# Mixture-of-experts weights: bias folded from row sums on GpSimd and VectorE instead of column sums on TensorE

## Chip, cores and metric

The kernel runs on 1 core of one Trainium2 chip. The metric is the device time of one execution in microseconds (us). Engines are called as in the profile: PE is TensorE, DVE is VectorE, ACT is ScalarE, POOL is GpSimd, SP is SyncE, which here only issues DMAs.

## The reference

64 batches of 256 tokens of width 256 pass through two residual layers: x1 = x + LN(att(LN(x), ctx) + LN(x))·gamma + beta, with attention without softmax (per head k'v from 120 context rows, then q·kv), and then

```
h2   = layernorm(x1)
top2 = top-2 of softmax(h2 @ gate_w.T)            # 16 experts
y_e  = relu(h2 @ expert_w[e].T + expert_b[e])     # expert_w: 16 x 256 x 256, float32
out  = x1 + sum over the two experts of weight * y_e
```

## The kernel before

**Two parts.** The dense part (to about 475 us) treats one batch per step. The second part (two passes of 144 tiles of 128 rows) gathers rows sorted by expert, multiplies each tile with its expert's matrix and scatters the result. Only the dense part's code is touched, with one wait count at the head of the second.

**The bias fold.** The rows that the expert matrices multiply are not the normalised h2 but rows of x1 shifted by `sigma - mean` (L873, L882). They sum to 256·sigma, so a vector u added to every row of an expert's matrix adds 256·sigma·u to its product. The kernel adds u = (bias - column sums of the matrix)/256, which brings the bias in and takes the shift out. So each expert's `we` (128 partitions x 2 halves x 256 columns; `we` holds all 16 side by side) needs its column sums over 256 rows, spread over 128 partitions, then one addition. After it the matrix is split for fp32r products: `we_head` is the rounded copy (ACT, L934), `we_rest` the difference, written over `we` (POOL, L573).

**How it is staged.** Every engine has its own in-order program, `step(s)`, called for s = 0, 1, ... (or from -1); semaphores hold the engines together, and nothing is reordered. In a step each engine works on several batches at once: `s` is in projection, `s-1` in attention, `s-2` in the second layernorm, `s-3` (called `f`) in expert choice and scatter. The order in `step` is the order on the engine. POOL's step `s` waits for x1 of batch `s-1` (L552), that is for the end of DVE's step `s`, so it runs beside DVE's step `s+1`. It does `context_rest(s+1)` (c_rest, L543), `x_beta` (L558), the small copies L582 to L587, and two indirect DMAs that scatter batch f's rows (L594). Between x_beta and the small copies stand the two pieces of the weights' preparation below.

**The weights' preparation,** in 8 pieces of 2 experts, one piece per step:
- SP loads pieces 0 to 3 in step 0 and 4 to 7 in step 1 (L394), 512 KB each.
- POOL adds the two halves of a piece (`we_sum`, L568), in steps 1 to 8.
- PE, in `sum_columns` (L732, steps 2 to 9), multiplies by a matrix of -1 (which sums over partitions and spreads the sum to all) and, by a matrix of ones, the bias in three bf16 parts (`be_rows`), into `ps_fold`, which is the bank of the transposes of h. So `transpose_h` waits for the fold of the step before (L656).
- DVE, in `fold_bias` (L1113, steps 3 to 10), adds ps_fold/256 to the piece.
- ACT makes the head in steps 3 to 10 (L934), POOL the rest in steps 4 to 11 (L573).
- The bias parts are made at the start: DVE clears `be_rows` (L977) and splits the bias (L979), SP writes them to DRAM and reads them back as rows (L385, L389), with waits in SP's queue.

**Functions and lines that the change and the prediction touch:** `prepare_experts` and `load` of SP; POOL's `step` (L549 to L598); PE's `transpose_h`, `sum_columns`, `step`; ACT's `step` (L932 to L934); DVE's `split`, `fold_bias`, `step`. Other DVE work of a step that the prediction names: moments L993, scores L1006, gaps L1016, onehot L1028, attention plus residual L1070, kv L1076, scaled L1090, first weights L1042, and x1 L1103, the last.

Of the kernel before, what the change touches and what calls it, by code (L numbers as in the profile page):

```python
# [25 lines left out]
P = 128  # L26
# [3 lines left out]
E = 16  # L30
# [24 lines left out]
WARM_TABLE, WARM_LOADS, WARM_BOUNDARY = 16, 20, 36  # L55
WE_PIECES = 8
RB = 4
LOG_EXP_SET = 6
# [80 lines left out]

def build(nc, x, ctx_t, wkv_t, wq_t, gate_t, we_t, bkv, be, bq, gamma, beta, out):  # L140
    bins = [nc.dram_tensor("bins0", [ROWS, ROW], F32, kind="Internal").ap(),
            nc.dram_tensor("bins1", [DUMP + 2 * E * P, FULL], F32, kind="Internal").ap()]

    be_dram = nc.dram_tensor("be_dram", [3, E * D], BF16, kind="Internal").ap()

    def parts_as_rows(dram):
        return dram.rearrange("n (p m) -> p n m", p=P)

    with ExitStack() as ctx:
        def sb(name, shape, dt=F32):  # L150
            return ctx.enter_context(nc.sbuf_tensor(name, shape, dt))
# [28 lines left out]
        we_rest = we[:].bitcast(F32R)  # L180
        we_sum = sb("we_sum", [P, 2, E * D // WE_PIECES])
        idle = sb("idle", [P, 2 * D], BF16)
        kv_bias = sb("kv_bias", [SC, 2 * D])
        be_in = sb("be_in", [P, E * D // P])
        be_rest = sb("be_rest", [P, 2, E * D // P])
        be_part = sb("be_part", [P, 3, E * D // P], BF16)
        bq_sb = sb("bq_sb", [P, KC])
# [55 lines left out]
        wkv = row_flat[:, 0:4 * D].rearrange("p (c n) -> p c n", c=KC)  # L243
        be_rows = row_flat[:, 4 * D:4 * D + E * D // 2].bitcast(BF16)
        put_at = sb("put_at", [P, V], I32)
# [24 lines left out]
        s_wrest = sem("weight_rests_ready")  # L270
        s_whalf = sem("weight_halves_added")
        s_wsum = sem("weight_column_sums_ready")
        s_fold = sem("weights_with_bias_ready")
# [6 lines left out]
        s_zero = sem("zeros_made")  # L280
        s_split = sem("bias_split_step")
        s_eb = sem("expert_bias_rows_placed")
        s_ebd = sem("expert_bias_parts_in_dram")
        s_init = sem("dram_fill_written")
# [70 lines left out]
        def piece(n):  # L355
            return slice(n * E * D // WE_PIECES, (n + 1) * E * D // WE_PIECES)

        block = ctx.enter_context(nc.Block())


        @block.sync
        def _(sp):
# [20 lines left out]
            load(Batch(2))  # L383
            sp.wait_ge(s_split, 5)
            sp.dma_start(parts_as_rows(be_dram), be_part[:]).then_inc(s_ebd, 16)  # L385
            load(Batch(3))
            sp.wait_ge(s_zero, 3)
            sp.wait_ge(s_ebd, 16)
            sp.dma_start(be_rows[0:65:32, :], be_dram).then_inc(s_eb, 16)  # L389

            def prepare_experts(step):

                for n in pieces(step, 4):
                    sp.dma_start(we[:, :, piece(n)],  # L394
                                 we_t.rearrange("(c p) n -> p c n", p=P)[:, :, piece(n)]
                                 ).then_inc(s_we[n], 16)
                if step >= LEAD - 4:

                    sp.wait_ge(s_const, 2)
                    q = step - (LEAD - 4)  # L400
                    spare = bins[0][SPARE + 4 * q * P:SPARE + 4 * (q + 1) * P, :].rearrange("(j p) d -> p j d", p=P)
                    sp.dma_start(spare[:, :, 0:D], zeros[:, 0:D].unsqueeze(1).to_broadcast([P, 4, D])
                                 ).then_inc(s_init, 16)
                    sp.dma_start(spare[:, :, D:ROW], pad_facts[:, 1, 4 * q:4 * q + 4, :]).then_inc(s_init, 16)
                if step == LEAD - 5:

                    sp.wait_ge(s_const, 2)
                    regions = bins[0][0:SPARE, :].rearrange("(r n) d -> n r d", n=REGION)
                    facts = pad_facts[:, 0].rearrange("p (r o) d -> p r o d", o=2)
                    for o, ends in enumerate((regions[0:PAD], regions[REGION - PAD:REGION])):  # L410
                        sp.dma_start(ends[:, :, 0:D], zeros[:, 0:D].unsqueeze(1).to_broadcast([P, E // 2, D])
                                     ).then_inc(s_init, 16)
                        sp.dma_start(ends[:, :, D:ROW], facts[:, :, o, :]).then_inc(s_init, 16)
# [69 lines left out]
        def _(pool):  # L483
# [63 lines left out]
            context_rest(Batch(0))  # L547

            def step(s):  # L549
                p = s - 1  # L550
# [10 lines left out]
                if s.c == 0:  # L561
                    make_pads()
                if s.c >= 1:
                    for n in pieces(s.c - 1, 1):
                        pool.wait_ge(s_we[n], 16)
                        if n >= 2:
                            pool.wait_ge(s_wsum, n - 1)
                        pool.tensor_tensor(we_sum[:, n % 2], we[:, 0, piece(n)], we[:, 1, piece(n)],  # L568
                                           ALU.add).then_inc(s_whalf, 1)
                if s.c >= 4:  # L570
                    for n in pieces(s.c - 4, 1):
                        pool.wait_ge(s_whead, n + 1)
                        pool.tensor_tensor(we_rest[:, :, piece(n)], we[:, :, piece(n)],  # L573
                                           we_head[:, :, piece(n)].bitcast(F32),
                                           ALU.subtract).then_inc(s_wrest, 1)
                f = s - 3
                if f.exists():
# [15 lines left out]
                    for t in range(NT):  # L593
# [3 lines left out]
                                ap=r[:, t, POS_COL:POS_COL + 1].bitcast(I32), axis=0),  # L597
                            in_offset=None).then_inc(s_row[f.buf(4)], 16)  # L598

            dense_steps(step, 0, NB + 3)  # L600
# [18 lines left out]
        def _(pe):  # L619
# [29 lines left out]
            def transpose_h(b):  # L649
# [3 lines left out]
                if b.c >= 2:  # L653
                    pe.wait_ge(s_gfold, 1)
                if b.c >= 3:
                    pe.wait_ge(s_fold, min(b.c - 2, WE_PIECES))  # L656
                for c in range(KC):
# [73 lines left out]

            def sum_columns(n, b):  # L732
                pe.wait_ge(s_whalf, n + 1)
                pe.wait_ge(s_ht, b.times(1, 1))
                if n == 0:
                    pe.wait_ge(s_eb, 16)
                pe.matmul(ps_fold, ones_bf[:], be_rows[:, piece(n)], start=True, stop=False)
                pe.matmul(ps_fold, minus_ones[:], we_sum[:, n % 2], start=False, stop=True).then_inc(s_wsum, 1)

            def step(s):  # L740
# [13 lines left out]
                if s.c == 1:  # L754
                    sum_gate_columns(s)
                if s.c >= 2:
                    for n in pieces(s.c - 2, 1):
                        sum_columns(n, s)
                if (s - 2).exists():
# [54 lines left out]

            pe.wait_ge(s_wrest, WE_PIECES)
            for k in range(2):
# [9 lines left out]
        def _(act):  # L826
# [80 lines left out]
            def step(s):  # L907
# [23 lines left out]

                for n in pieces(s.c - 3, 1):  # L932
                    act.wait_ge(s_fold, n + 1)
                    act.activation(we_head[:, :, piece(n)], we[:, :, piece(n)], ACT.Copy).then_inc(s_whead, 1)  # L934

# [38 lines left out]
        def _(dve):  # L974
            dve.memset(eps[:], EPS).then_inc(s_zero, 1)
            dve.memset(idle[:].bitcast(U32), 0).then_inc(s_zero, 1)
            dve.memset(be_rows.bitcast(U32), 0).then_inc(s_zero, 1)  # L977

            def split(src, rest, part, n):  # L979

                dve.tensor_copy(part[:, 0, :], src).then_inc(s_split, 1)
                dve.wait_ge(s_split, n + 1)
                dve.tensor_tensor(rest[:, 0, :], src, part[:, 0, :], ALU.subtract).then_inc(s_split, 1)
                dve.wait_ge(s_split, n + 2)
                dve.tensor_copy(part[:, 1, :], rest[:, 0, :]).then_inc(s_split, 1)
                dve.wait_ge(s_split, n + 3)
                dve.tensor_tensor(rest[:, 1, :], rest[:, 0, :], part[:, 1, :], ALU.subtract).then_inc(s_split, 1)
                dve.wait_ge(s_split, n + 4)
                dve.tensor_copy(part[:, 2, :], rest[:, 1, :]).then_inc(s_split, 1)

# [121 lines left out]

            def fold_bias(n):  # L1113
                dve.wait_ge(s_wsum, n + 1)
                part = we[:, :, piece(n)]
                dve.scalar_tensor_tensor(out=part, in0=ps_fold.unsqueeze(1).to_broadcast([P, KC, 2 * D]),
                                         scalar=1.0 / D, in1=part, op0=ALU.mult, op1=ALU.add).then_inc(s_fold, 1)

            def step(s):
# [7 lines left out]
                if s.c == 2:  # L1127
                    centre_gate()
                if s.c >= 3:
                    for n in pieces(s.c - 3, 1):  # L1130
                        fold_bias(n)
                if b.exists():
# [43 lines left out]

            dve.wait_ge(s_be_in, 16)
            split(be_in[:], be_rest, be_part, 0)
            dense_steps(step, -1, NB + 3)


# [132 lines left out]
```

## Time and profile before

| | us |
|---|---|
| median of 3 runs | 890.44 (888.53 to 893.2) |
| profiled execution, span from first to last instruction | 888.4 |
| PE, DVE, ACT, POOL busy in it | 756.4, 684.9, 593.1, 602.5 |
| dense part, first scores to last | about 24 to 475 |

The profiled execution's own time is shown as its span alone; it lies 2.0 us below the median of the runs. A row of a timeline gives start, duration, engine, line, operation, output<-input with shapes, the count of merged instructions, and in brackets the engine's idle time before it and what ended it. Records of one engine overlap by some tens of nanoseconds, since the next instruction is taken up before the last has drained.

### The profile page before, as it was taken

To read this page: it belongs to the slowest core of one execution; us is meant where nothing else is said; L and a number is where in the kernel's file an instruction comes from. 1 tells how busy PE (TensorE), PEld (TensorE's weight loads), DVE (VectorE), ACT (ScalarE), POOL (GpSimd) and SP (SyncE) were. 2 spreads that over 40 slices of the span, in tenths; PEclk is the share of its full clock that TensorE was granted. 3 is DMA by queue.
4 is the path that set the end of the run, shared out by engine and by line. 5 is a ranking of instruction groups with operands and counts; after the bars stand their busy time and mean duration, and the time that the engine had idled before them with its cause. 6 is when DMAs were issued, how large, how long until landed. Compare 5 with 4: busy or idle time off the path is not lost.

```text
span 888.4 us, 21064 instructions
## 1 busy us (share of the span) xinstructions
PE 756.4 (85%) x5479; PEld 659.0 (74%) x5480; DVE 684.9 (77%) x2219; ACT 593.1 (67%) x1658; POOL 602.5 (68%) x776
## 2 busy tenths in 40 slices
PE   5998899999999999999988777787777899777750
PEld 4866688888888888888875777786665898667750
DVE  4989999999999999999994767777662575554540
ACT  4877789989989989889872545555452565454440
POOL 4578766666666666666662777777774677777775
PEclk9999999999999999999997999999998999999995
DMA  7426456676676776676513898999996999999941
GB/s 241 151 71 166 148 184 207 219 238 203 222 237 200 227 234 202 223 236 199 197 50 99 283 307 297 310 300 310 303 303 203 350 363 343 302 305 293 305 154 77
DMA packets 137626, 205.77 MB, mean 232 GB/s; under 512 B 38962, under 2 KB 74290, under 8 KB 137546
## 3 DMA queue, kind: packets, MB, share of 16 engines
q1 hardware_dynamic: 113101, 130.72, 47.7%
q0 software_dynamic: 24448, 74.14, 22.3%
q8 instruction: 34, 0.56, 0.3%
q14 instruction: 43, 0.35, 0.1%
HBM read 87.99 MB, written 116.81 MB: 231 GB/s over the span
## 4 chain that ended last, share of the span: by engine, by line
DVE 37%; issue 24%; POOL 11%; PE 11%; DMA 10%; SPq 4%; ACT 1%; POOLq 0%; DVEq 0%; ACTq 0%
POOL out_rows L609 8%; DVE st L993 6%; DVE x L1103 6%; DVE scaled L1090 5%; DVE att L1070 4%; DMA row_in<-bins 4%; DMA bins<-row_in,put_at 4%; DVE kv L1076 4%; POOL bins L609 3%; DVE top_i L1023 3%; DMA out_rows<-xh,put_at 2%; DVE scores_top L1011 2%; SPq L459 2%; PE ps_q L679 1%; DVE scores_top L1006 1%
## 5 line engine op out<-in xcount | busy, mean ns | idle before, releaser
L609 POOL DMA_INDIRECT out_rows<-xh,put_at x143 | 145.2, 1015 | 57.6 <-issue 39.9
L609 POOL DMA_INDIRECT bins<-row_in,put_at x143 | 143.8, 1006 | 57.7 <-issue 37.9
L594 POOL DMA_INDIRECT bins<-rows x128 | 127.1, 993 | 72.0 <-POOL rows L587 47.5
L679 PE MATMUL ps_q<-h_t,wq 128*128 128x256 f32 x512 | 133.3, 383 | 0.0
L543 POOL TENSOR_TENSOR c_rest<-c_sb,c_head 128x240 fp32r<-128x240 f32 x64 | 44.8, 700 | 87.2 <-DVE x L1103 84.1
L679 PEld LDWEIGHTS ps_q<-h_t,wq 128*128 128x128 f32 x512 | 92.8, 191 | 13.6 <-ACT h_t L899 0.4
L798 PE MATMUL ps_q<-we_head,row_head 128*128 x288 | 87.3, 303 | 8.6 <-DVE row_rest L1234 8.6
L1261 DVE SCALAR_TENSOR_TENSOR row_in<-row_in 128x256 f32<-128x256 f32 x144 | 63.3, 480 | 28.8 <-ACT row_in L955 28.2
L858 ACT ACTIVATE q_t<-ps_q,bq_sb 128x256 f32<-128x256 f32 x128 | 60.4, 472 | 36.5 <-PE ps_q L679 36.5
L558 POOL TENSOR_TENSOR x_beta<-xh,beta_sb 128x512 f32<-128x512 f32 x64 | 81.9, 1280 | 0.8 <-DVE x L1103 0.8
L701 PEld LDWEIGHTS ps_mg<-wg_centred,h_t 128*128 128x128 f32 x512 | 64.4, 196 | 22.7 <-issue 20.7
L799 PE MATMUL ps_q<-we_head,row_rest 128*128 x288 | 80.7, 280 | 0.0
L800 PE MATMUL ps_q<-we,row_head 128*128 x288 | 80.6, 280 | 0.0
L645 PE MATMUL ps_att<-kvm,q_t 128*128 128x128 f32 x512 | 72.8, 285 | 0.8 <-ACT q_t L858 0.8
L1265 DVE COPY put_at<-row_in 128x2 int32<-128x2 int32 x72 | 14.0, 194 | 76.8 <-ACT xh L955 76.7
L891 ACT ACTIVATE xh<-xh,nmr,rstd 128x256 f32<-128x256 f32 x128 | 69.2, 589 | 0.2 <-DVE nmr L999 0.2
L701 PE MATMUL ps_mg<-wg_centred,h_t 128*128 128x16 f32 x512 | 67.4, 264 | 1.4 <-ACT h_t L905 1.4
L798 PEld LDWEIGHTS ps_q<-we_head,row_head 128*128 128x128 f32 x288 | 55.1, 191 | 12.4 <-issue 12.2
L645 PEld LDWEIGHTS ps_att<-kvm,q_t 128*128 128x128 f32 x512 | 62.3, 192 | 1.3 <-ACT q_t L858 1.3
L845 ACT ACTIVATE lnv<-st,eps 128x2 f32<-128x2 f32 x192 | 55.0, 287 | 9.1 <-DVE st L993 8.8
L882 ACT ACTIVATE rows<-x,rows 128x256 f32<-128x256 f32 x128 | 58.1, 501 | 2.1
L1103 DVE SCALAR_TENSOR_TENSOR x<-scaled,rstd,x_beta 128x256 f32<-128x256 f32 x128 | 56.3, 481 | 1.4 <-issue 0.4
(169 smaller groups left out, 2401.3 us busy)
## 6 DMA issues: line engine op xcount, KB each, us to landing
bins<-zeros SPq DMA_DIRECT2D x48, 768.0 KB, 4.6
row_in<-bins SPq DMA_DIRECT2D x128, 260.0 KB, 4.0
row_in<-bins SPq DMA_DIRECT2D x160, 132.0 KB, 2.3
xh<-in_x SPq DMA_DIRECT2D x64, 256.0 KB, 2.8
c_sb<-in_ctx_t SPq DMA_DIRECT2D x64, 120.0 KB, 2.8
we<-in_we_t SPq DMA_DIRECT2D x8, 512.0 KB, 6.5
bins<-row_in,put_at POOLq DMA_INDIRECT x143, 3.9
out_rows<-xh,put_at POOLq DMA_INDIRECT x143, 4.5
```

Of the source, the lines that this page charges most:

```text
L558: pool.tensor_tensor(x_beta[:, n], x_sb[:, s.buf(4)], beta_sb[:].unsqueeze(1).to_broadcast([P, NT, D]), ALU.add).then_inc(s_xb, 1)
L594: pool.indirect_dma_start(out=bins[0], in_=r[:, t, :], out_offset=bass.IndirectOffsetOnAxis(ap=r[:, t, POS_COL:POS_COL + 1].bitcast(I32), ...
L609: pool.indirect_dma_start(out=bins[1] if k == 0 else out, in_=row_in[:, t, :] if k == 0 else y[:, t, :], out_offset=bass.IndirectOffsetOnA ...
L645: mm = pe.matmul(ps_att[:, t, c * P:(c + 1) * P], q_t[:, c, t, :], kvm[:, c, :], start=True, stop=True)
L679: mm = pe.matmul(ps_q[dc][:, 0:S], wq[:, c, dc * P:(dc + 1) * P], h_t[:, c, :, :], start=(c == 0), stop=(c == KC - 1))
L701: mm = pe.matmul(logits[:, t, :], h2_t[:, c, t, :], wg_centred[:, c, :], start=(c == 0), stop=(c == KC - 1))
L798: pe.matmul(o, heads, w_head, start=(c == 0), stop=False)
L799: pe.matmul(o, rests, w_head, start=False, stop=False)
L800: mm = pe.matmul(o, heads, we_rest[:, c, bass.ds(at[2 * j + t], D)], start=False, stop=(c == KC - 1))
L891: a = act.activation(h[:, b.buf(4), t, :], x_sb[:, b.buf(4), t, :], ACT.Identity, bias=nmr[:, t:t + 1], scale=rstd[:, 0, b.buf(2), t:t + 1])
L1103: dve.scalar_tensor_tensor(out=x1[:, b.buf(2), t, :], in0=scaled[:, t, :], scalar=rstd[:, 1, b.buf(2), t:t + 1], in1=x_beta[:, b.buf(2), t ...
L1261: at = dve.scalar_tensor_tensor(out=row_in[:, t, 0:D], in0=row_in[:, t, D:2 * D], scalar=row_in[:, t, D + S_COL:D + S_COL + 1], in1=row_in ...
```

## The change

The host passes the expert weights a second time, as `we_d`, in rows of the matrices' output index, so that a matrix's column sum becomes the sum along one row.

- **SP**: the round trip of the bias parts is gone. After `load(3)` it loads seven pieces of `we_d` (512 KB each, 4 rows of 256 per partition) into a ring in `row_in`, and the eighth in step 2 after a wait. The 8 pieces of `we` move from steps 0 and 1 to steps 4 and 5. In step 7 it writes (bias - sums)/256 to DRAM (16 KB), in step 8 it reads that to all 128 partitions (`be_all`, 2 MB).
- **POOL**: `quarter(n)` halves each row twice (two tensor_tensor, output 128x512 and 128x256), pieces 0 to 3 in step 0, 4 and 5 in step 1, 6 in step 2, 7 in step 3. `we_sum` is gone. At the **end** of POOL's step, after the two indirect DMAs, stand now: in steps 10, 13, ..., 55 the addition of `be_all` to one expert (output 128x512), and in steps 12, 15, ..., 57 the rest of one expert (128x512).
- **DVE**: `fold_bias` (8), the split (5) and the memset are gone; 8 tensor_reduce (128x4 from 128x256; 4, 2, 1 and 1 in steps 2 to 5) and two operations on 128x32 in step 6 are new.
- **PE**: the 24 matmuls of `sum_columns` and the wait of `transpose_h` for the fold are gone.
- **ACT**: the heads are made one expert at a time, 16 times 128x512, in steps 11, 14, ..., 56.

```diff
+SUM_RING = 7
+FIRST_FOLD, FOLD_STEPS = 10, 3
-        be_rows = row_flat[:, 4 * D:4 * D + E * D // 2].bitcast(BF16)
+        we_by_row = row_flat[:, 4 * D:4 * D + SUM_RING * 4 * D].rearrange("p (r m j) -> p r m j", r=SUM_RING, j=D)
+        be_all = row_flat[:, 4 * D:4 * D + E * D]
...
+        def first_pieces(step):
+            return {0: range(0, 4), 1: range(4, 6), 2: range(6, 7), 3: range(7, 8)}.get(step, range(0))
+        def expert_at(step, after):
+            e, odd = divmod(step - FIRST_FOLD - after, FOLD_STEPS)
+            return range(e, e + 1) if odd == 0 and 0 <= e < E else range(0)
...
-            sp.wait_ge(s_split, 5)
-            sp.dma_start(parts_as_rows(be_dram), be_part[:]).then_inc(s_ebd, 16)
             load(Batch(3))
-            sp.wait_ge(s_zero, 3)
-            sp.wait_ge(s_ebd, 16)
-            sp.dma_start(be_rows[0:65:32, :], be_dram).then_inc(s_eb, 16)
+            def load_by_row(n):
+                if n >= SUM_RING:
+                    sp.wait_ge(s_wsum, n - SUM_RING + 1)
+                sp.dma_start(we_by_row[:, n % SUM_RING], by_row[:, n]).then_inc(s_wd[n % SUM_RING], 16)
+            for n in range(SUM_RING):
+                load_by_row(n)
             def prepare_experts(step):
-                for n in pieces(step, 4):
+                if step == 2:
+                    load_by_row(SUM_RING)
+                if step == FIRST_FOLD - 3:
+                    sp.wait_ge(s_less, 2)
+                    sp.dma_start(be_dram.rearrange("(p m) -> p m", p=P), be_less[:, 1]).then_inc(s_ebd, 16)
+                if step == FIRST_FOLD - 2:
+                    sp.wait_ge(s_ebd, 16)
+                    sp.dma_start(be_all, be_dram.partition_broadcast(P)).then_inc(s_eb, 16)
+                for n in pieces(step - 4, 4):
...
+            def quarter(n):
+                part = we_by_row[:, n % SUM_RING]
+                pool.wait_ge(s_wd[n % SUM_RING], 16 * (n // SUM_RING + 1))
+                pool.tensor_tensor(part[:, :, 0:D // 2], part[:, :, 0:D // 2], part[:, :, D // 2:D],
+                                   ALU.add).then_inc(s_whalf, 1)
+                pool.wait_ge(s_whalf, n + 1)
+                pool.tensor_tensor(part[:, :, 0:D // 4], part[:, :, 0:D // 4], part[:, :, D // 4:D // 2],
+                                   ALU.add).then_inc(s_wquart, 1)
             def step(s):
-                if s.c >= 1:
-                    for n in pieces(s.c - 1, 1):
...
+                for n in first_pieces(s.c):
+                    quarter(n)
                 f = s - 3
...
+                for e in expert_at(s.c, 0):
+                    if e == 0:
+                        pool.wait_ge(s_eb, 16)
+                    if e % 2 == 0:
+                        pool.wait_ge(s_we[e // 2], 16)
+                    pool.tensor_tensor(we[:, :, expert(e)], we[:, :, expert(e)],
+                                       be_all[:, expert(e)].unsqueeze(1).to_broadcast([P, KC, D]),
+                                       ALU.add).then_inc(s_fold, 1)
+                for e in expert_at(s.c, 2):
+                    pool.wait_ge(s_whead, e + 1)
+                    pool.tensor_tensor(we_rest[:, :, expert(e)], we[:, :, expert(e)],
+                                       we_head[:, :, expert(e)].bitcast(F32), ALU.subtract).then_inc(s_wrest, 1)
...
-                if b.c >= 3:
-                    pe.wait_ge(s_fold, min(b.c - 2, WE_PIECES))
-                if s.c >= 2:
-                    for n in pieces(s.c - 2, 1):
-                        sum_columns(n, s)
-            pe.wait_ge(s_wrest, WE_PIECES)
+            pe.wait_ge(s_wrest, E)
...
-                for n in pieces(s.c - 3, 1):
-                    act.wait_ge(s_fold, n + 1)
-                    act.activation(we_head[:, :, piece(n)], we[:, :, piece(n)], ACT.Copy).then_inc(s_whead, 1)
+                for e in expert_at(s.c, 1):
+                    act.wait_ge(s_fold, e + 1)
+                    act.activation(we_head[:, :, expert(e)], we[:, :, expert(e)], ACT.Copy).then_inc(s_whead, 1)
...
-            dve.memset(be_rows.bitcast(U32), 0).then_inc(s_zero, 1)
-            split(be_in[:], be_rest, be_part, 0)
-                    for n in pieces(s.c - 3, 1):
-                        fold_bias(n)
+            def sum_rows_of_weights(n):
+                dve.wait_ge(s_wquart, n + 1)
+                dve.tensor_reduce(w_sums[:, 4 * n:4 * n + 4], we_by_row[:, n % SUM_RING, :, 0:D // 4], AX_X,
+                                  ALU.add).then_inc(s_wsum, 1)
+                for n in first_pieces(s.c - 2):
+                    sum_rows_of_weights(n)
+                if s.c == FIRST_FOLD - 4:
+                    bias_less_sums()
```

## Rows read from the trace of the kernel before

**Rows 1.** By stretch: length; busy PE, PEld, DVE, ACT, POOL; PE clock, DMA share, GB/s
```profile
48.00:60.00 12.00, 10.46 (x59) 7.86 (x58) 10.10 (x31) 7.67 (x24) 10.29 (x11) 0.86 0.28 86
122.00:455.00 333.00, 332.59 (x2402) 287.96 (x2401) 328.30 (x1250) 300.55 (x950) 216.78 (x352) 1.00 0.65 213
```
**Rows 2.** Timeline of DVE: end of one steady step and start of the next
```profile
131.81 0.20 DVE L1063 TENSOR_REDUCE rows<-picked 128x4 int32<-128x64 f32 x1
131.92 0.16 DVE L1042 TENSOR_TENSOR rows<-inverse,rstd 128x2 f32<-128x2 f32 x1
132.10 0.88 DVE L1103 SCALAR_TENSOR_TENSOR x<-scaled,rstd,x_beta 128x256 f32<-128x256 f32 x2
133.01 0.70 DVE L993 BATCH_NORM_STATS2 st<-x 128x6 f32<-128x512 f32 x1
...
134.91 0.17 DVE L1016 TENSOR_TENSOR gaps<-scores_top 128x36 f32<-128x36 f32 x1
```
**Rows 3.** Timeline of POOL over the same steady step
```profile
129.57 1.00 POOL L594 DMA_INDIRECT bins<-rows  x1 [0.77 <-POOL rows L587]
130.87 0.96 POOL L594 DMA_INDIRECT bins<-rows  x1 [0.30 <-issue]
133.07 0.69 POOL L543 TENSOR_TENSOR c_rest<-c_sb,c_head 128x240 fp32r<-128x240 f32 x1 [1.23 <-DVE x L1103]
133.72 1.28 POOL L558 TENSOR_TENSOR x_beta<-xh,beta_sb 128x512 f32<-128x512 f32 x1
```
**Rows 4.** Timeline: POOL's long operation and DVE's onehot while it runs
```profile
69.01 2.38 POOL L573 TENSOR_TENSOR we<-we,we_head 128x1024 fp32r<-128x1024 f32 x1
...
69.08 0.69 DVE L1070 TENSOR_TENSOR att<-ps_att,xh 128x512 f32<-128x512 f32 x1
69.68 1.78 DVE L1028 TENSOR_TENSOR onehot<-iota_e,top_i 128x64 bf16<-128x64 f32 x1
```
**Rows 5.** The view of line L1028: shortest, median and longest in ns
```profile
L1028 DVE TENSOR_TENSOR onehot<-iota_e,top_i x64: 207/214/1807, 34.2 to 472.1; 128x64 bf16<-128x64 f32 x64
```
**Rows 6.** Timeline of DVE: attention plus residual (L1070), once a step, at three places
```profile
24.93 0.69 DVE L1070 TENSOR_TENSOR att<-ps_att,xh 128x512 f32<-128x512 f32 x1
...
128.38 0.68 DVE L1070 TENSOR_TENSOR att<-ps_att,xh 128x512 f32<-128x512 f32 x1
...
135.01 0.68 DVE L1070 TENSOR_TENSOR att<-ps_att,xh 128x512 f32<-128x512 f32 x1
```
**Rows 7.** The chain that ended last: L1070 in four steps between them
```profile
49.51 0.60 DVE att L1070
...
61.25 0.60 DVE att L1070
...
105.32 0.60 DVE att L1070
...
113.56 0.60 DVE att L1070
```
**Rows 8.** Timeline: a step in which POOL came late to c_rest
```profile
437.82 0.88 DVE L1103 SCALAR_TENSOR_TENSOR x<-scaled,rstd,x_beta 128x256 f32<-128x256 f32 x2
...
439.57 0.70 POOL L543 TENSOR_TENSOR c_rest<-c_sb,c_head 128x240 fp32r<-128x240 f32 x1
...
440.64 0.94 DVE L1016 TENSOR_TENSOR gaps<-scores_top 128x36 f32<-128x36 f32 x1
```
**Rows 9.** Groups by line: busy us, mean ns of one, idle before
```profile
L573 POOL TENSOR_TENSOR we<-we,we_head 128x1024 fp32r<-128x1024 f32 x8 | 19.0, 2374 | 0.0
L899 ACT ACTIVATE h_t<-ps_ht 128x512 f32<-128x512 f32 x64 | 38.2, 597 | 4.9 <-PE ps_ht L659 0.9
```
**Rows 10.** Timeline: the first c_rest and the DVE operation beside it
```profile
8.95 1.22 DVE L1123 TENSOR_TENSOR wkv_rest<-row_in,wkv_head 128x1024 fp32r<-128x1024 f32 x1
...
9.62 1.11 POOL L543 TENSOR_TENSOR c_rest<-c_sb,c_head 128x240 fp32r<-128x240 f32 x1 [2.35 <-DMA wg<-in_gate_t]
```
**Rows 11.** DMA issues: KB each, median us to landing
```profile
we<-in_we_t SPq DMA_DIRECT2D x8, 512.0 KB, 6.5
```

More of the change, by code:

```diff
@@ L56 @@
 WE_PIECES = 8
+ROW_CHUNKS = E * D // P
+SUM_RING = 7
+FIRST_FOLD, FOLD_STEPS = 10, 3
 RB = 4
@@ L137, in table_reader, with build @@
     return read
-def build(nc, x, ctx_t, wkv_t, wq_t, gate_t, we_t, bkv, be, bq, gamma, beta, out):
+def build(nc, x, ctx_t, wkv_t, wq_t, gate_t, we_t, we_d, bkv, be, bq, gamma, beta, out):
     bins = [nc.dram_tensor("bins0", [ROWS, ROW], F32, kind="Internal").ap(),
             nc.dram_tensor("bins1", [DUMP + 2 * E * P, FULL], F32, kind="Internal").ap()]
-    be_dram = nc.dram_tensor("be_dram", [3, E * D], BF16, kind="Internal").ap()
-    def parts_as_rows(dram):
-        return dram.rearrange("n (p m) -> p n m", p=P)
+    be_dram = nc.dram_tensor("be_dram", [E * D], F32, kind="Internal").ap()
     with ExitStack() as ctx:
@@ L180, in build @@
         we_rest = we[:].bitcast(F32R)
-        we_sum = sb("we_sum", [P, 2, E * D // WE_PIECES])
         idle = sb("idle", [P, 2 * D], BF16)
         kv_bias = sb("kv_bias", [SC, 2 * D])
-        be_in = sb("be_in", [P, E * D // P])
-        be_rest = sb("be_rest", [P, 2, E * D // P])
-        be_part = sb("be_part", [P, 3, E * D // P], BF16)
+        be_in = sb("be_in", [P, ROW_CHUNKS])
+        w_sums = sb("w_sums", [P, ROW_CHUNKS])
+        be_less = sb("be_less", [P, 2, ROW_CHUNKS])
         bq_sb = sb("bq_sb", [P, KC])
@@ L270, in build @@
         s_wrest = sem("weight_rests_ready")
-        s_whalf = sem("weight_halves_added")
-        s_wsum = sem("weight_column_sums_ready")
+        s_wd = [sem(f"weights_by_row_loaded{n}") for n in range(SUM_RING)]
+        s_whalf = sem("weight_rows_halved")
+        s_wquart = sem("weight_rows_quartered")
+        s_wsum = sem("weight_row_sums_ready")
+        s_less = sem("bias_less_sums_step")
         s_fold = sem("weights_with_bias_ready")
@@ L280, in build @@
         s_zero = sem("zeros_made")
-        s_split = sem("bias_split_step")
-        s_eb = sem("expert_bias_rows_placed")
-        s_ebd = sem("expert_bias_parts_in_dram")
+        s_eb = sem("expert_bias_spread")
+        s_ebd = sem("expert_bias_in_dram")
         s_init = sem("dram_fill_written")
@@ L356, in piece, with expert @@
             return slice(n * E * D // WE_PIECES, (n + 1) * E * D // WE_PIECES)
+        def first_pieces(step):
[3 more added lines that the diff above has]
+            return range(e, e + 1) if odd == 0 and 0 <= e < E else range(0)
+        def expert(e):
+            return slice(e * D, (e + 1) * D)
         block = ctx.enter_context(nc.Block())
@@ L383, in _ @@
             load(Batch(2))
-            sp.wait_ge(s_split, 5)
-            sp.dma_start(parts_as_rows(be_dram), be_part[:]).then_inc(s_ebd, 16)
             load(Batch(3))
-            sp.wait_ge(s_zero, 3)
-            sp.wait_ge(s_ebd, 16)
-            sp.dma_start(be_rows[0:65:32, :], be_dram).then_inc(s_eb, 16)
-            def prepare_experts(step):
-                for n in pieces(step, 4):
+            by_row = we_d.rearrange("(p r m) j -> p r m j", p=P, m=4)
+            def load_by_row(n):
[4 more added lines that the diff above has]
+                load_by_row(n)
+            def prepare_experts(step):
+                if step == 2:
[7 more added lines that the diff above has]
+                for n in pieces(step - 4, 4):
                     sp.dma_start(we[:, :, piece(n)],
@@ L562, in step @@
                     make_pads()
-                if s.c >= 1:
-                    for n in pieces(s.c - 1, 1):
[L565 to L575, printed above, removed]
+                for n in first_pieces(s.c):
+                    quarter(n)
                 f = s - 3
@@ L730, in sum_gate_columns @@
                 mm.then_inc(s_gsum, 1)
[L732 to L738, printed above, removed]
             def step(s):
@@ L976, in _ @@
             dve.memset(idle[:].bitcast(U32), 0).then_inc(s_zero, 1)
-            dve.memset(be_rows.bitcast(U32), 0).then_inc(s_zero, 1)
[L979 to L989, printed above, removed]
             def moments(n, b, src):
@@ L1111, in centre_gate, with bias_less_sums @@
                                          scalar=1.0 / D, in1=wg[:], op0=ALU.mult, op1=ALU.add).then_inc(s_gfold, 1)
[L1113 to L1117, printed above, removed]
+            def sum_rows_of_weights(n):
+                dve.wait_ge(s_wquart, n + 1)
+                dve.tensor_reduce(w_sums[:, 4 * n:4 * n + 4], we_by_row[:, n % SUM_RING, :, 0:D // 4], AX_X,
+                                  ALU.add).then_inc(s_wsum, 1)
+            def bias_less_sums():
+                dve.wait_ge(s_wsum, WE_PIECES)
+                dve.wait_ge(s_be_in, 16)
+                dve.tensor_tensor(be_less[:, 0], be_in[:], w_sums[:], ALU.subtract).then_inc(s_less, 1)
+                dve.wait_ge(s_less, 1)
+                dve.tensor_scalar(be_less[:, 1], be_less[:, 0], 1.0 / D, None, ALU.mult).then_inc(s_less, 1)
             def step(s):
@@ L1128, in step @@
                     centre_gate()
-                if s.c >= 3:
-                    for n in pieces(s.c - 3, 1):
-                        fold_bias(n)
+                for n in first_pieces(s.c - 2):
+                    sum_rows_of_weights(n)
+                if s.c == FIRST_FOLD - 4:
+                    bias_less_sums()
                 if b.exists():
@@ L1175, in step @@
                     finish_x1(p)
-            dve.wait_ge(s_be_in, 16)
-            split(be_in[:], be_rest, be_part, 0)
             dense_steps(step, -1, NB + 3)
@@ L1300 @@
         "we_t": c(g["expert_w"].transpose(2, 0, 1).reshape(D, E * D)),
+        "we_d": c(g["expert_w"].reshape(E * D, D)),
         "bkv": c(np.concatenate([g["bk"], g["bv"]])),
```

## The prediction

> **What bounds the kernel now.** I read the busy times first, then stretches, then single steps. By the page DVE is busy 684.9 and POOL 602.5 of 888.4 us, which says little, since the parts differ. The stretch from 122 to 455 us, 50 steps of the dense part, shows DVE busy 328.3 of 333.0 us, PE 332.6 (its ends are modelled, and it is pipelined), ACT 300.6 and POOL 216.8 [rows 1]. There a step takes 135.01 - 128.38 = 6.63 us [rows 6], and DVE's list of work fills it to within 0.1 us. Whatever DVE gains or loses in such a step moves the end by the same amount. POOL looks free: it waits 1.23 us per step between its second scatter (ends at 130.87 + 0.96 = 131.83) and x1 (c_rest starts at 133.07) [rows 3]. The change fills just this hole.
>
> **A second bound hides between POOL and DVE.** At 69.01 POOL starts an operation of 2.38 us, which ends at 71.39. DVE's onehot, taken up at 69.68, lasts 1.78 us [rows 4], to 71.46; its median is 0.21 [rows 5]. It was held until POOL had done. L1070 just before it ran its usual 0.69 beside the same operation [rows 4, 6]; it reads one input from PSUM and one from SBUF, onehot reads both from SBUF. From 105.32 to 113.56 is a step in which we_rest is the only extra work: 8.24 us [rows 7], 1.61 over 6.63. So a hold of DVE goes into the end in full. The hold works the other way too: at 9.62 POOL's c_rest, the first, took 1.11 us [rows 10] instead of about 0.69 [rows 3], ending 0.56 after DVE's two-SBUF-input L1123 was done at 10.17. The Trainium skill ("SBUF — State Buffer", section "Who interferes with whom") states it as a lock: a VectorE instruction with two SBUF inputs and a GpSimd instruction that reads SBUF exclude each other for a whole instruction, whoever comes first. By that rule, the trace agrees. With it the sum is the one worked out below from the rows; without it, by POOL's waiting time alone, it would be the first rival's.
>
> **What goes.** The preparation in its old form costs the early steps. From the second L1070 at 24.93 to the one at 128.38 there are 12 steps in 103.45 us [rows 6]; 12 x 6.63 = 79.6, so 23.9 us are excess: eight folds on DVE with PE's sums before them, holds like the one above, and one step of 11.74 us (49.51 to 61.25 [rows 7]) in which the PE clock stood at 1.2 GHz for a while (0.86 over 48 to 60 [rows 1]). All of it goes: **-23.9**. The split, the memset and the bias DMAs at the start are removed before DVE and SP are needed; I cost them at nothing, since the chain starts with the loads of x and wkv.
>
> **What comes early.** Eight reduces of 256 elements: bounds 0.20 (place, 64 elements) and 0.70 (moments, 512) [rows 2], I take 0.35, as 256 lies between: 2.8. Two operations on 32 elements: 0.4. POOL's quarters: an output of 512 elements takes 1.28, 240 takes 0.69 [rows 3], so 256 takes 0.73, and a piece 2.0 us. Four pieces in step 0 are hidden under POOL's wait for the first x1 (they end about 23 us if the loads run at the 213 GB/s of [rows 1], and before them POOL sat idle), but may hold scaled or x1 of the first batch. Those of steps 1 to 3 stand behind x_beta. They end 2.0 us after x_beta, where onehot wants to start 0.6 after it, so they hold DVE about 1.4 us in two steps and about 1 in another; bounds for all quarters together 0 and 8, I take 4.0. Early in sum **+7.2**, net **-16.7** (bounds -21 and -12).
>
> **What comes late.** 16 additions and 16 rests of 128x512 on POOL. Duration: 1.28 for x_beta [rows 3], the same size, and 2.37 for the double size [rows 9], so 1.28 each. Each stands behind the second scatter, so it starts at 131.83 to 131.9. DVE's next operations are first weights (L1042, taken up at 131.92, behind place, which ends at 132.01) and x1 (132.10 to 132.98) [rows 2]; both read two SBUF inputs. POOL is there first: DVE is held to about 131.9 + 1.28 = 133.18 where it wanted 131.98. That is 1.2 us per operation. If first weights is quicker by some hundredths, POOL gets in behind it at 132.08 and holds x1 to 133.36 instead of 132.15, 1.2 us again. After it x1 is late, POOL waits for it as before, and the next step starts with the old phase; nothing catches up, because DVE has only 0.1 us to spare. All 32 fall in steps 10 to 57, all steady. **32 x 1.2 = +38.4** (bounds 1.05 and 1.35: 34 and 43).
>
> **What I cost at nothing.** ACT's 16 heads of 0.60 (as L899 [rows 9]) stand in the steps whose x1 is 1.2 us late; ACT then waits for moments and has this time. Without the holds it would have only 32.4/50 = 0.65 us per step [rows 1], in several pieces, and up to 0.2 would reach DVE 16 times (3 us). PE's 24 matmuls are in the 23.9 already. SP's waits: the sum of piece 0 (step 2), the bias (step 7) and the write's landing (step 8) are older than the x_beta that SP's load waits for in the same step; queued behind them are the batch loads, four steps ahead. The 2 MB of be_all have 16 us from step 8 to the end of POOL's step 10; four loads of 512 KB took 6.5 us each to landing [rows 11], issued together about 10 us. If it's late, POOL waits once, a few us. The moved loads of we have five steps. The second part is unchanged.
>
> **Sum.** Against the profiled execution: 888.4 - 16.7 + 38.4 = 910.1. The span lies 2.0 below the median of the runs, so 912.1, say **912 us**.
>
> **Rivals.**
> 1. *The hole takes them.* DVE is not held at the end of a step (scatter records on POOL are rough, POOL's operation might run beside x1), and 1.28 us of work goes into 1.23 of waiting. Then only the early gain and ACT's 3 us are left: 890.4 - 16.7 + 3 = 877, or 873 if the quarters don't hold either. For it: POOL is idle 116 us in the stretch [rows 1]. Against it: [rows 4, 10]. It decides if a hold costs under 0.3 us. Chance 0.11.
> 2. *POOL is the one that waits.* DVE keeps the read for first weights and both x1, POOL's operation runs from 132.98 to 134.26, c_rest is 1.2 late and x_beta too. This happens once before: c_rest starts at 439.57, 0.87 after x1 was done at 438.70, and gaps takes 0.94 instead of 0.17, until 441.58, when the x_beta behind that c_rest (0.66 + 1.28 later) has ended [rows 8]. At 1.2 late the same gives 1.2, which is my number on another path. But gaps (134.91) might slip in between c_rest and x_beta; then onehot alone is held, 0.75 us: 890.4 - 16.7 + 24 = 898. Chance 0.10.
> 3. *More than the holds.* Longer steps leave PE idle, and the clock falls as between 48 and 60 us [rows 1]; that step took 11.74 [rows 7], some 3 us above the mean of the twelve, 8.6. Five such, or be_all late, give 927. Against it: one drop in these twelve steps. Chance 0.12.
>
> My forecast has the rest, 0.67. Its own range is 903 to 923 (the bounds of both terms, not all at once). The range for 8 in 10 leaves out the first rival and part of the third, and takes in the second: 892 to 926. A difference under 0.5% (4.5 us) can't be told from none here. Faster by more: 0.12, the first rival and a little of the second. Within: 0.04, from the second. Slower: 0.84.
>
> **What would show it.** (a) L1042 or L1103 has 32 records of about 1.4 to 1.7 us, in steps with POOL's we operations, others unchanged; steps of 7.85 us twice in three, and 6.6 between. (b) If POOL's own operation or gaps has the long records, it is the second rival. (c) If L1042, L1103, L1016 and L1028 keep their durations, I am wrong and the first rival holds. (d) The L1070 that stood at 105.32 comes before any of the 32 operations; 9 steps after the one at 24.9, with 9 x 6.63 + 7.2 it should stand near 92. (e) No long wait of SP on the sums, none of POOL on be_all, ACT's heads without waiting.

## The result, and the profile after

The changed kernel takes 905.53 us (median of 4 runs, 903.66 to 907.15) against 890.79 for the kernel before in the same comparison: a ratio of 1.016, 95% interval 1.0133 to 1.0188. It is slower by 14.7 us, where 912 (892 to 926) was forecast. The profiled execution took 907.15 us, 905.4 of them its span; the span before was 888.4.

The same stretch as in [rows 1], and the two groups of late operations on POOL with the DVE instruction that follows them (busy us, mean ns of one, idle before):
```profile
122.00:455.00 333.00, 318.28 (x2205) 264.87 (x2204) 329.58 (x1149) 278.56 (x888) 235.34 (x348) 1.00 0.63 202
```
```profile
L634 POOL TENSOR_TENSOR we<-we,we_head 128x512 fp32r<-128x512 f32 x16 | 20.4, 1276 | 0.4
L629 POOL TENSOR_TENSOR we<-we,row_in 128x512 f32<-128x512 f32 x16 | 20.4, 1275 | 0.4
L1053 DVE TENSOR_TENSOR rows<-inverse,rstd 128x2 f32<-128x2 f32 x64 | 44.6, 697 | 0.0
```
DVE is as busy as before, 329.6 of 333 us, but it issues 1149 instructions in this time and not 1250. PE fell from 332.6 to 318.3. So DVE's busy time has grown without work. The place is L1053, first weights (L1042 before): 64 of them took 44.6 us, where 64 x 0.16 is 10. The timeline shows one held step and the free one behind it, first DVE, then POOL:
```profile
95.33 1.25 DVE L1053 TENSOR_TENSOR rows<-inverse,rstd 128x2 f32<-128x2 f32 x1
96.50 0.87 DVE L1114 SCALAR_TENSOR_TENSOR x<-scaled,rstd,x_beta 128x256 f32<-128x256 f32 x2
...
99.40 0.69 DVE L1081 TENSOR_TENSOR att<-ps_att,xh 128x512 f32<-128x512 f32 x1
...
102.95 0.16 DVE L1053 TENSOR_TENSOR rows<-inverse,rstd 128x2 f32<-128x2 f32 x1
103.12 0.88 DVE L1114 SCALAR_TENSOR_TENSOR x<-scaled,rstd,x_beta 128x256 f32<-128x256 f32 x2
```
```profile
94.29 0.96 POOL L619 DMA_INDIRECT bins<-rows  x1 [0.30 <-issue]
95.27 1.28 POOL L629 TENSOR_TENSOR we<-we,row_in 128x512 f32<-128x512 f32 x1
97.45 0.69 POOL L569 TENSOR_TENSOR c_rest<-c_sb,c_head 128x240 fp32r<-128x240 f32 x1 [0.90 <-DVE x L1114]
```
POOL's addition begins 0.02 us after the second scatter and ends at 96.55; DVE's instruction on 128x2 elements, taken up at 95.33, lasts until 96.58. Behind the hold x1 is taken up 1.17 us after first weights, 0.17 in the free step. POOL still waits for x1 for 0.90 us. Over the whole dense part exactly 32 of the 64 records of L1053 are long (1.16 to 1.25 us), one beside each of the 32 operations.

Where the 17.0 us of span came from, by DVE's attention plus residual (L1070 before, L1081 after):

| | before | after | difference |
|---|---|---|---|
| eleventh one starts | 105.2 | 91.8 | -13.4 |
| from it to the last (53 steps) | 355.6 | 382.8 | +27.3 |
| from there to the end | 427.6 | 430.7 | +3.1 |

The second line holds 32 steps of 7.60 where 6.63 was (+31.0), less the two holds of the old rests (8.25 and 8.26) that fell in it (-3.2), and less about 0.5 of single longer steps of the kernel before (one of 7.00). The third is code that did not change.

### The profile page after: what moved, and what is told of

It reads as the page before. It is cut to its first block, busy times and chain, and to the rows that moved or that the text cites. A ratio compares the mean times of both kernels' runs of the same rounds, so it can differ in the third digit from the quotient of the medians.

```text
span 905.4 us, 20986 instructions
## 1 busy us (share of the span) xinstructions
PE 766.8 (85%) x5455; PEld 662.5 (73%) x5456; DVE 699.8 (77%) x2215; ACT 587.5 (65%) x1666; POOL 629.1 (69%) x808
## 4 chain that ended last, share of the span: by engine, by line
DVE 38%; issue 29%; POOL 11%; DMA 10%; PE 6%; SPq 2%; ACT 2%; POOLq 0%; DVEq 0%; ACTq 0%
POOL out_rows L646 7%; DVE x L1114 6%; DVE scaled L1101 6%; POOL bins L646 5%; DVE att L1081 4%; DVE st L1004 4%; DMA row_in<-bins 3%; DMA out_rows<-xh,put_at 3%; DMA bins<-row_in,put_at 3%; DVE kv L1087 3%; DVE top_i L1034 2%; DVE scores_top L1022 2%; SPq L485 2%; DVE scores_top L1017 1%; DVE picked L1064 1%
## 5 line engine op out<-in xcount | busy, mean ns | idle before, releaser
L670 PE MATMUL ps_kv<-wkv_head,c_head 128*120 128x512 f32 x128 | 56.8, 444 | 11.4 <-POOL c_rest L569 11.4
```

## The experiments

**The late operations cut to a few elements.** Each works on 2 columns a half, the rests likewise; the expert matrices stay without bias and the rests unfinished. The additions' line, cut (the rests' likewise):
```diff
-                    pool.tensor_tensor(we[:, :, expert(e)], we[:, :, expert(e)],
+                    pool.tensor_tensor(we[:, :, few(e)], we[:, :, few(e)],
...
```


> The 32 late operations stay where they are, but each works on 2 x 2 elements instead of 2 x 256 (the expert matrices stay without bias and the rests unfinished). Theory (GpSimd's operation holds VectorE's first two-input instruction, 0.97 us a time): an operation of 0.19 us holds for 0.1 us at most, so 905.5 - 31 + 0 to 3 = 874 to 878 us, and L1053 (first weights) back at 0.16 us in all steps. Rival (the 31 us have another source: ScalarE's heads, the transfers, GpSimd's waits): well above 885.

Measured: 873.87 us (869.96 to 876.01), before 889.45 beside it, ratio 0.9815 (0.9775 to 0.9855). First weights in all steps:
```profile
L1056 DVE TENSOR_TENSOR rows<-inverse,rstd 128x2 f32<-128x2 f32 x64 | 10.4, 162 | 0.0
```
The 31 us are the duration of these operations, not the heads, the transfers or the waits. A small rest shows too, in the timeline of attention plus residual:
```profile
98.66 0.68 DVE L1084 TENSOR_TENSOR att<-ps_att,xh 128x512 f32<-128x512 f32 x1
...
105.45 0.68 DVE L1084 TENSOR_TENSOR att<-ps_att,xh 128x512 f32<-128x512 f32 x1
...
112.08 0.68 DVE L1084 TENSOR_TENSOR att<-ps_att,xh 128x512 f32<-128x512 f32 x1
```
Every third step takes 6.79 us and not 6.63. The small operations come in two steps of three, ACT's heads in one of three. The first head runs at 97.36, ACT then works without a pause, and in the step from 98.66 DVE's nmr is taken up 2.08 us after attention and not 1.94. So I put this 16 x 0.16 = 2.6 us to the heads; no run takes them out alone.

**The same time on POOL without a read.** A memset of the same length stands for each operation, and bias and rests are left out (the arguments are cut here):
```diff
-                    pool.tensor_tensor(we[:, :, expert(e)], ...).then_inc(s_fold, 1)
+                    pool.memset(row_flat[:, 20 * D:20 * D + 1410], 0.0).then_inc(s_fold, 1)
-                    pool.tensor_tensor(we_rest[:, :, expert(e)], ...).then_inc(s_wrest, 1)
+                    pool.memset(row_flat[:, 20 * D:20 * D + 1410], 0.0).then_inc(s_wrest, 1)
```


> The 32 late operations are replaced by a memset of 128x1410 in unused space, which should take 1.28 us as they did (0.53 us for 512, 0.31 for 256 elements before), so it writes SBUF and reads nothing; bias and rests are left out. Theory (the hold is on SBUF reads): VectorE isn't held, 875 to 881 us, with c_rest up to 0.1 us late. First rival (whatever GpSimd does holds a two-input instruction of VectorE): 905. Second rival (the length of GpSimd's step costs, since c_rest comes late): 905 with L1053 at 0.16 and GpSimd never waiting.

Measured: 873.69 us (871.89 to 874.95), ratio 0.9832 (0.9803 to 0.9861). POOL's timeline:
```profile
93.26 0.96 POOL L619 DMA_INDIRECT bins<-rows  x1 [0.30 <-issue]
94.21 1.29 POOL L629 MEMSET row_in<- 128x1410 f32 x1
95.46 0.70 POOL L569 TENSOR_TENSOR c_rest<-c_sb,c_head 128x240 fp32r<-128x240 f32 x1
```
POOL is occupied for 1.29 us at the same place, doesn't wait for x1 at all any more, and the kernel loses nothing by it (873.87 with the operations of a few elements). So neither the length of POOL's step nor its occupation costs; what costs is that an operation of POOL which reads SBUF meets an instruction of DVE with two SBUF inputs. The Trainium skill ("SBUF — State Buffer", "Who interferes with whom") says that one which only writes does not collide with such an instruction; this pair of runs shows it.

**The same work at three other places of POOL's step.** First behind the onehot, ahead of the scatters:
```diff
                     if f.c < NB - 1:
                         pool.wait_ge(s_w0, f.times(1, 1))
                         pool.tensor_tensor(r[:, :, W1_COL], ...)
+                    if any(expert_at(s.c, after) for after in (0, 2)):
+                        pool.wait_ge(s_oh, f.times(1, 2))
+                    for e in expert_at(s.c, 0):
...
+                    for e in expert_at(s.c, 2):
...
```


> All 32 operations in full, but placed behind the small copies and ahead of the two scatters, after a wait for the onehot that runs at that time on VectorE. Theory: VectorE reads two SBUF inputs next in nmr, 1.1 us after onehot, so each operation of 1.28 us holds it for about 0.25 us: 905.5 - 31 + 8 = 883 (880 to 888). Rival (GpSimd's longer step costs, wherever the work stands): 903 to 908.

Measured: 879.19 us (878.49 to 881.74), before 889.45, ratio 0.9886 (0.9861 to 0.9912), with the whole computation. One step, POOL and then DVE:
```profile
106.82 1.27 POOL L625 TENSOR_TENSOR we<-we,we_head 128x512 fp32r<-128x512 f32 x1 [0.48 <-DVE onehot L1041]
```
```profile
107.86 0.25 DVE L1012 SCALAR_TENSOR_TENSOR nmr<-st,rstd 128x2 f32<-128x2 f32 x1
```
The rest ends at 108.09; nmr (two SBUF inputs) takes 0.25 and not 0.15. Between onehot and nmr stand moments (one input) and kv (one of its two from PSUM), and those run beside POOL freely. The steps with an operation take 6.80 us; 0.10 of the 0.17 over 6.63 is nmr's, the rest I did not trace. The third step, without an operation, takes 6.63, so the 0.16 of the kernel above doesn't show there. The first operation costs more: it begins only at 93.64, and scaled beside it takes 1.76 instead of 0.86 us, in a step of 7.61. SP issued be_all's load at 82.84, and it took 10.7 us to land; earlier in the step than in the change, the first addition comes before it.

Second, directly behind x_beta, where the kernel before had its own:

> All 32 operations in full, directly behind x_beta, where the kernel before had its own. Theory: gaps, which starts when x_beta ends, is held for the whole operation, about 1.2 us instead of 0.97: 905.5 + 7 = 912 (907 to 916), gaps at 1.3 to 1.4 us in 32 steps and L1053 at 0.16. Rival (only GpSimd's length counts): 905.

Measured: 895.11 us (892.94 to 895.92), ratio 1.0071 (1.0045 to 1.0097). The direction against the place of the change was expected wrongly: this is 10 us faster, not 7 slower. POOL and DVE of one step:
```profile
104.63 1.28 POOL L594 TENSOR_TENSOR x_beta<-xh,beta_sb 128x512 f32<-128x512 f32 x1
105.88 1.28 POOL L611 TENSOR_TENSOR we<-we,we_head 128x512 fp32r<-128x512 f32 x1
```
```profile
105.82 0.18 DVE L1027 TENSOR_TENSOR gaps<-scores_top 128x36 f32<-128x36 f32 x1
...
106.52 0.72 DVE L1039 TENSOR_TENSOR onehot<-iota_e,top_i 128x64 bf16<-128x64 f32 x1
```
Gaps was taken up at 105.82, 0.09 us before x_beta's recorded end, as in [rows 2, 3], and 0.06 before POOL's next operation; it takes its usual 0.18. So not gaps but onehot is held, for 0.5 us of the 1.28. The hold is as the theory says; which instruction it hits hangs on hundredths of a microsecond. Some 2 of the 21 us that this place costs over the memset run are the first step's (8.58 us), in which POOL waited 1.73 us for be_all and then held nmr for 0.9, and the late x_beta held gaps for 0.9.

Third, at the end of the step as in the change, but only after x1:
```diff
+                if expert_at(s.c, 0) or expert_at(s.c, 2):
+                    pool.wait_ge(s_x1, s.times(NT, NT))
```


> The 32 late operations where the change put them, but each waits for the x1 that VectorE makes last in the step, so that first weights and x1 are not held and the operation runs ahead of c_rest. Theory: now c_rest and x_beta come 1.2 us late, and x_beta holds gaps (1.2 to 1.3 us) or, if gaps slips in before it, onehot (0.65): 874.5 + 32 x 0.65 to 1.3 = 895 to 916, and L1053 at 0.16. Rival (only a late x1 costs): 875 to 880.

Measured: 897.36 us (894.09 to 898.22), ratio 1.0088 (1.006 to 1.0116). First weights is free, but now c_rest comes behind the operation, and with it x_beta. POOL and DVE:
```profile
110.53 1.27 POOL L636 TENSOR_TENSOR we<-we,we_head 128x512 fp32r<-128x512 f32 x1 [1.23 <-DVE x L1116]
111.76 0.69 POOL L569 TENSOR_TENSOR c_rest<-c_sb,c_head 128x240 fp32r<-128x240 f32 x1
112.41 1.30 POOL L594 TENSOR_TENSOR x_beta<-xh,beta_sb 128x512 f32<-128x512 f32 x1
```
```profile
112.37 0.18 DVE L1029 TENSOR_TENSOR gaps<-scores_top 128x36 f32<-128x36 f32 x1
...
113.07 0.73 DVE L1041 TENSOR_TENSOR onehot<-iota_e,top_i 128x64 bf16<-128x64 f32 x1
```
Gaps slips in between c_rest and x_beta and onehot is held, to 113.8. This is the second rival of the prediction, made on purpose; it costs 0.5 us by the hold and, in steps of 7.3 to 7.5, 0.2 to 0.3 more. Between 100 and 400 us PE waited for c_rest 28 times, up to 0.7 us, and DVE's nmr for ACT's rstd 14 times, 0.2 each; that the first causes the second is likely, but not shown.
```profile
PE ps_kv L672 <- POOL c_rest L569: 17.5, 28, 0.7
```

**Operations that fit the gap.** 22 additions and 22 rests of 192 columns (the last of 64) behind the onehot, one in each of 44 steps (cut):
```diff
-FIRST_FOLD, FOLD_STEPS = 10, 3
+FIRST_FOLD, FOLD_STEPS = 10, 2
+CHUNK, CHUNKS = 192, 22
...
+        def chunk(n):
+            return slice(n * CHUNK, min((n + 1) * CHUNK, E * D))
```


> As e3_behind_onehot, but in 22 additions and 22 rests of 192 columns (384 elements a partition, about 1.0 us each) in place of 32 operations of 1.28 us, one in each of 44 steps. Theory: an operation that begins after onehot and ends before nmr begins, 1.1 us later, holds nothing; so the 5 us that e3 still pays go: 879.2 - 5 = 874 us (872 to 877), nmr at 0.15 us. Rival (each operation on GpSimd costs by its number or by the sum of its time, 44 us here instead of 41): 879 or more.

Measured: 873.74 us (872.6 to 874.6), before 889.39 beside it, ratio 0.9831 (0.9805 to 0.9857), with the whole computation. POOL, and the group of nmr behind it:
```profile
105.99 1.00 POOL L625 TENSOR_TENSOR we<-we,row_in 128x384 f32<-128x384 f32 x1 [0.48 <-DVE onehot L1046]
```
```profile
107.03 0.15 DVE L1017 SCALAR_TENSOR_TENSOR nmr<-st,rstd 128x2 f32<-128x2 f32 x1
```
The operation ends at 106.99, nmr starts at 107.03. More operations and more time on POOL, 43 us against 41, cost nothing that the medians show against the runs with a few elements (873.87) and with memsets (873.69). Only the first operation, late at 92.84, held nmr for 0.7 us.

**The early part.** In the changed kernel, POOL's halvings of the first steps cut to one element per row, so that the columns are not summed:
```diff
-                pool.tensor_tensor(part[:, :, 0:D // 2], part[:, :, 0:D // 2], part[:, :, D // 2:D],
+                pool.tensor_tensor(part[:, :, 0:1], part[:, :, 0:1], part[:, :, D // 2:D // 2 + 1],
```


> The changed kernel with the early halvings on GpSimd (16 operations in steps 0 to 3) cut to one element per row, so that the column sums are wrong; the 32 late operations as they were. Theory: the early halvings hold VectorE for 3 to 4 us in all (nmr, scaled, gaps, onehot in steps 1 to 4), so 905.5 - 3.5 = 902 (900 to 904). Rival (the early part is set by the loads and the reduces): 905.

Measured: 900.87 us (898.44 to 900.99), ratio 1.0126 (1.0093 to 1.0158). The first ten steps of attention plus residual take 88.06 - 19.62 = 68.4 us; in the changed kernel 91.8 - 19.9 = 71.9. So 3.4 us of the early time are holds by the halvings. The six experiments' kernels with the halvings in full at their old place take 71.6 to 73.0 for this stretch, so single profiles give 3.1 to 4.5. The records of the changed kernel show which instructions were held; onehot hardly is (0.31 us twice):
```profile
22.41 0.62 DVE L1010 SCALAR_TENSOR_TENSOR nmr<-st,rstd 128x2 f32<-128x2 f32 x1
22.96 1.34 DVE L1101 SCALAR_TENSOR_TENSOR scaled<-att,st,gamma_sb 128x256 f32<-128x256 f32 x2
...
43.19 1.17 DVE L1027 TENSOR_TENSOR gaps<-scores_top 128x36 f32<-128x36 f32 x1
```

Then the kernel of chunks with the halvings of pieces 4 to 7 moved behind the onehot too, one operation a step (steps 3 to 10), FIRST_FOLD at 17:

> As e5_chunks, and the early halvings of pieces 4 to 7 stand behind the onehot too, one operation a step in steps 3 to 10, so that the fold begins in step 17. Theory: of the early holds those of steps 1 to 3, 2.5 us, go, and four halvings of 1.28 us cost 0.16 each: 2 us less than e5_chunks, 872. Rival (the early holds cost nothing in the end): as e5_chunks, 874.

Measured: 871.57 us (870.55 to 874.43), before 889.39, ratio 0.981 (0.9781 to 0.9839). The eleventh attention starts at 88.6 and not 91.1, as expected, but the runs of the two kernels overlap, so the end doesn't show the 2 us surely. Both beat both kernels of this case.

**What the kernel before paid for.** Its operations on POOL (we_sum and rests) cut to four columns, all folds on PE and DVE left (the sums and rests are left unfinished):

> The kernel before with its 16 early GpSimd operations on the weights cut to a few elements (column sums and rests wrong), all folds of TensorE and VectorE left as they were. This splits the 23.9 us of early excess. Theory: holds of onehot and gaps are 6 x 1.57 + 0.58 + 1.07 = 11 us of it, the rest is the folds' own time on VectorE (9.8 us) and waits for TensorE: 889.5 - 11 = 878 us (876 to 881), and the stretch from the second to the fourteenth attention-plus-residual falls from 103.5 to about 92. Rival (the folds on VectorE and TensorE are nearly all of the excess): 885 or more.

Measured: 878.39 us (875.35 to 879.06), ratio 0.9853 (0.9823 to 0.9883). The second and the fourteenth attention plus residual, to be held against [rows 6]:
```profile
25.17 0.69 DVE L1074 TENSOR_TENSOR att<-ps_att,xh 128x512 f32<-128x512 f32 x1
...
116.31 0.68 DVE L1074 TENSOR_TENSOR att<-ps_att,xh 128x512 f32<-128x512 f32 x1
```
91.1 us against 103.5. So 12.3 of the 23.9 us of early excess go with POOL's operations. The records held in the kernel before and free here, six onehots and two gaps, add up to 11.1 us. In the step of 11.74 (7.9 here) they are 2.1 of 3.8; there DVE also waits 1.85 us for a column sum of PE, whose granted clock was 0.78 from 52 to 55 us and 0.65 from 55 to 58, after it had been busy for only 1.9 of the 3 us before:
```profile
57.45 1.23 DVE L1116 SCALAR_TENSOR_TENSOR we<-ps_ht,we 128x1024 f32<-128x1024 f32 x1 [1.85 <-PE ps_ht L738]
```
The other 11.6 us belong to the folds; 9.8 of them are DVE's own eight operations of 1.23, and no run separates the share of TensorE's sums in the rest. So the kernel before paid about as much for the holds as for the folds.

## Why the prediction was right

- **What bounds.** Right: DVE's list of work sets the step. The undisturbed steps of the changed kernel take 6.63 us as in [rows 6], and a held one is later by the hold.
- **The second bound.** Right, and shown by two runs that differ in whether POOL reads: the same 1.28 us cost 0.97 a time as a read (the change) and nothing as a memset.
- **What goes, -23.9, and what comes early, +7.2.** The forecast put the L1070 that stood at 105.32 "near 92"; it starts at 91.8. That the 7.2 came out to the tenth is partly luck. With the halvings cut, the stretch to the eleventh is 68.4 us, 2.8 over 5.95 + 9 x 6.63; that is what the reduces and the two operations cost, where 3.2 was taken. The holds cost 3.4 by experiment, where 4.0 was taken, and they hit nmr, scaled and gaps, not onehot as forecast: the first halving begins before gaps does. The remaining 1.0 is a first attention at 19.9 instead of 19.0, which I had not foreseen; the other kernels with the same beginning have it at 18.3 to 19.3.
- **What comes late, 32 x 1.2 = +38.4.** The mis-sized term. Each cost 0.97, in all 31.0. The place was right (POOL is there first, L1042 waits), the duration was right (1.276 measured, 1.28 forecast). But I counted the start up to 0.07 after the scatter, where it was 0.02, and added the hold to the moment at which first weights could begin, although its own 0.1 us up to x1 was over almost with the hold: x1 is taken up 0.05 us before POOL's operation is recorded as ended. By [rows 2] I could have read the price as 131.85 + 1.28 - 0.05 - 132.10 = 0.98, from the start of x1 and not of first weights. 0.97 lies below my lower bound of 1.05. In the same way the signs of (a) came smaller than forecast: records of 1.16 to 1.25 us, not 1.4 to 1.7, and steps of 7.60, not 7.85.
- **At nothing.** ACT's heads cost nothing in the changed kernel, whose other steps take 6.63 us: behind the head at 97.13 ACT waits 0.40 us for moments. Without holds every third step is 0.16 longer, where I had said up to 0.2. SP shows no wait on the sums, and POOL none on be_all. The second part took 3.1 us more in the profiled execution. From the first rest of a row to the end, the profiles of this code in the eleven kernels differ between 400 and 407 us, so I take this as the spread of single executions; its cause was not looked for.
- **The sum.** In spans 910.1 was forecast and 905.4 measured: 7.4 too much for the holds, about 0.5 of single longer steps of the kernel before, and against them 3.1 not foreseen in the second part, which by luck hid part of the error. The other 1.9 of the 6.6 us between 912.1 and 905.5 is the step from span to median: 2.0 in the forecast, 0.1 now, since the profiled execution (907.15) lay above the median.
- **The rivals.** "The hole takes them" fell by the records of L1053, and would have been 874, as the memset run shows. "POOL is the one that waits" did not happen by itself; forced, it gave 897, against 898 worked out; the 0.75 us a time assumed there for onehot's hold was 0.5 of hold and 0.2 to 0.3 of other delay, so the agreement is partly luck. More drops of the clock were not seen: the mean granted clock is 0.966 in both profiles.

## What to carry to other kernels

Idle time of GpSimd is not free time when VectorE is the bound. For each operation planned there, write down VectorE's instructions beside it and mark those with two SBUF inputs; work that reads SBUF belongs into the stretches between them, cut to their length, and held there by a wait on the instruction that ends the last one. Here the same 41 us of GpSimd work cost 31 us at the end of the step, about 21 behind x_beta (2 of them by the wait for be_all), 5 behind the onehot (1 of them so) and nothing measurable in pieces of 1.0 us.

## What the runs showed that was not expected

- Two POOL operations in a row are not one long hold for DVE. Gaps, taken up 0.06 us before the rest (105.82 and 105.88) and 0.04 before x_beta (112.37 and 112.41), went ahead of them and took its usual 0.18. The expectation of 912 us for the place behind x_beta failed on this, at 895. But being taken up first is not enough at these distances. In the run behind the onehot, scaled is taken up at 21.73 between two halvings, 0.02 before the second, which still takes its full 1.27, while the two of scaled take 2.44 and not 0.86. What decides between them no run here shows:
```profile
21.07 0.72 POOL L582 TENSOR_TENSOR row_in<-row_in 128x256 f32<-128x256 f32 x1
21.75 1.27 POOL L579 TENSOR_TENSOR row_in<-row_in 128x512 f32<-128x512 f32 x1
```
```profile
21.73 2.44 DVE L1103 SCALAR_TENSOR_TENSOR scaled<-att,st,gamma_sb 128x256 f32<-128x256 f32 x2
```
- A hold costs less than the growth of the held record: the record grew from 0.16 to 1.24, by 1.08 us, and the step by 0.97.
